# Attention scores made once, and their probabilities turned by DMA: one core, sixteen sequences

## The reference

```python
x = x + einsum(x, weight[subject]) + bias[subject]       # one of 8 matrices
x = x + diffusion(x)                                      # neighbours in both directions, and x * (1 - x)
# attention: 16 heads of 16 features, queries from a side input, 256 keys from x, and one key of the query's own
score_prev = einsum('bhqd,bhkd->bhqk', q, k_prev) / 4     # masked past seq_len1
score_self = (q * k_self).sum(-1) / 4
weights = softmax(concat[score_prev, score_self])
x = x + (weights[:-1] @ v_prev + weights[-1] * v_self) @ Wo + bo
# experts: relu(x @ wi) @ wo for two shared experts and one of 3 chosen, mixed by a gate of 3
x = x + eo * w[0] + s0 * w[1] + s1 * w[2]
```

## Time and profile before

| what | value |
|---|---|
| median of the runs | 1002.32 us |
| the profiled execution's own time | 998.3 us |
| its span, first to last instruction | 995.7 us |
| mean granted TensorE clock | 0.997 |
| PE busy | 972.3 us (98%), 9659 matmuls |
| DVE busy | 796.9 us (80%) |
| ACT busy | 686.8 us (69%) |
| POOL busy | 635.9 us (64%) |
| DMA | 82.71 MB, mean 83 GB/s; queue q1 28.2% of the 16 engines' time |

### The profile page before, as it was taken

The page is one execution under the profiler, slowest core; times in us unless marked ns, Lnnn a source line. Parts: engine busy times, 40 slices in busy tenths (PEclk is TensorE's granted clock), DMA queues, the critical chain, the costliest instruction groups (busy, mean ns, idle before and its releaser), DMA issues.

```text
span 995.7 us, 28043 instructions
## 1 busy us (share of the span) xinstructions
PE 972.3 (98%) x9659; PEld 932.9 (94%) x9659; DVE 796.9 (80%) x1566; ACT 686.8 (69%) x1442; POOL 635.9 (64%) x544
## 2 busy tenths in 40 slices
PE   7889999999999999999999999999999999999997
PEld 7779999999999999999999999999999999999997
DVE  6877887888888787878888788788888878787754
ACT  5776858677685876768577685867768587676742
POOL 5867747576685757658565774757668575765541
PEclk9999999999999999999999999999999999999999
DMA  7443232313214231231413123231321423122110
GB/s 211 140 118 96 65 108 63 95 54 106 85 43 127 64 95 53 81 110 43 114 53 114 58 63 108 63 95 54 106 85 43 126 64 95 53 84 76 45 54 11
DMA packets 92029, 82.71 MB, mean 83 GB/s; under 512 B 12100, under 2 KB 90980, under 8 KB 92004
## 3 DMA queue, kind: packets, MB, share of 16 engines
q1 hardware_dynamic: 91572, 81.99, 28.2%
q10 hardware_dynamic: 432, 0.39, 0.1%
HBM read 52.59 MB, written 4.20 MB: 57 GB/s over the span
## 4 chain that ended last, share of the span: by engine, by line
PE 75%; POOL 9%; issue 8%; DVE 3%; ACT 3%; SPq 1%; DMA 1%; POOLq 0%; ACTq 0%; DVEq 0%
PE out L721 8%; PE out L722 8%; PE hid L721 8%; PE out L723 8%; PE hid L722 7%; PE hid L723 7%; PE front L847 4%; PE front L833 4%; PE front L721 4%; PE front L723 3%; PE front L722 3%; POOL prob_lo L1607 3%; POOL exp_lo L1543 2%; PE pv L788 2%; PE pv L789 2%
## 5 line engine op out<-in xcount | busy, mean ns | idle before, releaser
L721 PE MATMUL hid<-x_hi,exp_hi 128*128 128x256 f32 x768 | 230.6, 300 | 0.2
L721 PE MATMUL out<-hid_hi,exp_hi 128*128 128x256 f32 x768 | 229.0, 298 | 0.0
L1607 POOL TENSOR_TENSOR prob_lo<-prob,prob_hi 128x512 f16<-128x512 f32 x141 | 182.6, 1296 | 61.5 <-ACT prob_hi L1121 61.4
L722 PE MATMUL out<-hid_lo,exp_hi 128*128 128x256 f32 x768 | 217.3, 283 | 0.0
L723 PE MATMUL out<-hid_hi,exp_lo 128*128 128x256 f32 x768 | 216.8, 282 | 0.0
L722 PE MATMUL hid<-x_lo,exp_hi 128*128 128x256 f32 x768 | 216.5, 282 | 0.0
L723 PE MATMUL hid<-x_hi,exp_lo 128*128 128x256 f32 x768 | 216.2, 282 | 0.0
L1294 DVE TENSOR_REDUCE s_max<-front 128x2 f32<-128x512 f32 x247 | 163.5, 688 | 60.8 <-PE front L833 58.8
L1543 POOL TENSOR_TENSOR exp_lo<-raw,exp_hi 128x512 fp32r<-128x512 f32 x128 | 168.8, 1334 | 60.1 <-ACT exp_hi L1138 60.0
L1160 ACT ACTIVATE hid_hi<-hid 128x512 fp32r<-128x512 f32 x192 | 115.7, 603 | 101.2 <-PE hid L723 100.0
L1117 ACT ACTIVATE prob<-front 128x512 f32<-128x512 f32 x246 | 148.6, 604 | 24.2 <-PE front L847 20.6
(11 more groups left out here) (269 smaller groups left out, 2334.4 us busy)
## 6 DMA issues: line engine op xcount, KB each, us to landing
raw<-in_wi SPq DMA_DIRECT2D x64, 256.0 KB, 3.8
raw<-in_wo SPq DMA_DIRECT2D x64, 256.0 KB, 2.7
q_rows<-w_raw SPq DMA_DIRECT2D x80, 128.0 KB, 2.4
k_rows<-x_raw SPq DMA_DIRECT2D x48, 128.0 KB, 2.4
k_rows<-x1T SPq DMA_DIRECT2D x45, 128.0 KB, 2.3
x_raw<-in_x SPq DMA_DIRECT2D x16, 256.0 KB, 3.1
w_raw<-in_w SPq DMA_DIRECT2D x16, 256.0 KB, 2.7
s_raw<-in_side SPq DMA_DIRECT2D x16, 256.0 KB, 3.4
```

The source lines that it names most:

```text
L721: nc.tensor.matmul(acc, w_hi, a_hi, start=first, stop=False)
L722: nc.tensor.matmul(acc, w_hi, a_lo, start=False, stop=False)
L1607: nc.gpsimd.tensor_tensor(prob_lo[:, h % NPROB, :], prob[:, h % NPROB, :], prob_hi[:, h % NPROB, :], ALU.subtract).then_inc(prob_split_poo ...
```

## The change

- Stage E on PE, the maxima's way through PE, ScalarE and DMA (m0, m1, top0, top1) and pvend are gone.
- DVE takes the negated maximum of each head (L1294 before); ScalarE takes the exponential from the bank of stage S, with the query on the partitions and the maximum as its bias, in two halves of 256 columns. Stage C is a copy of prob (SBUF) to fp16. The factor 1/4 moves into the queries.
- SP stage T: for each head one transposing DMA of the high part (128 x 512, fp16) as soon as C is done, and one of the low part once that is made. There are three buffers of parts, and three of turned parts, one of them ksT's. Between its waits SP raises semaphores.
- `attend` is a PE stage V of its own, which waits for both DMAs.
- The maximum doesn't include the own score: own0 and own1 make two weights from the difference (one for the own term, one for all the others), and half, norm and att multiply by the second.
- All lists are in new orders. The opening has 190 idle matmuls in place of 132.

```diff
 PE_BODY = """
-H0 H1 S0 S1 P0 S2 S3 H2 S4 S5 P1 S6 S7 H3 S8 P2 m0 H4 S9 S10 P3 S11 H5
-E0 S12 P4 E1 S13 H6 E2 S14 P5 E3 S15 H7 E4 E5 P6 E6 H8 m1 E7
-x1 P7 q E8 H9 E9 lap P8 E10 E11 H10 E12 kp E13 P9 E14 E15 H11 P10 pvend P11
-vs aT ks gate wo logits vp self
+H0 H1 S0 S1 P0 H2 S2 P1 S3 H3 S4 P2 H4 S5 S6 V0 P3 H5 S7 V1 V2 P4 x1 S8 V3 H6 P5 S9 V4 S10 H7 V5 V6 q S11 P6 S12 V7 H8 P7 S13 S14 V8 V9
+H9 H10 S15 V10 P8 lap V11 V12 P9 H11 kp P10 V13 V14 V15 P11 vs aT ks gate wo logits vp self
...
 SP_BODY = """
-wo0 wo1 m0 wo2 wo3 m1 wi_load E15 kp k3 load sum
+T0 T1 T2 T3 wo0 T4 T5 T6 wo1 T7 T8 T9 wo2 T10 T11 T12 wo3 T13 T14 T15 kp k3 load wi_load sum
...
-NPROB = 3
+NPROB = 2
+NPARTS = 3
+NTURNED = 3
...
+                elif name[0] == "T":
+                    h = int(name[1:])
+                    if h == NTURNED - 1:
+                        wait_filled(sp, i, "self")
+                        sp.sem_inc(self_seen, 1)
+                    wait(sp, pv_done, H, i, max(h - NTURNED + 1, 0))
+                    sp.sem_inc(values_seen, 1)
+                    wait(sp, hi_done, H, i, h + 1)
+                    sp.sem_inc(hi_seen, 1)
+                    sp.dma_start(turned[h % NTURNED][:, 0:2 * C], prob_parts[:, h % NPARTS, 0], transpose=True).then_inc(turned_in[h % NPARTS], 16)
+                    wait_prob_split(sp, i, h)
+                    sp.sem_inc(parts_seen, 1)
+                    sp.dma_start(turned[h % NTURNED][:, 2 * C:4 * C], prob_parts[:, h % NPARTS, 1], transpose=True).then_inc(turned_in[h % NPARTS], 16)
...
             def attend(i, h):
 
-                wait_prob_split(pe, i, h)
+                wait_turned(pe, i, h)
...
-                    for k in range(C):
-                        last = nc.tensor.matmul(psum[:, k * S:(k + 1) * S], k_rows[0:ROWS_EXP, h, k * P:(k + 1) * P],
-                                                q_rows[0:ROWS_EXP, h, :], start=True, stop=True)
...
                 elif name[0] == "E":
                     h = int(name[1:])
-                    wait_filled(act, i, name)
+                    wait(act, max_done, H, i, h + 1)
                     if h >= NPROB:
                         wait_prob_split(act, i, h - NPROB)
-                    psum = front_psum(name, i)
-                    last = nc.scalar.activation(prob[:, h % NPROB, :], psum[:, :], ACT.Exp, scale=SCALE)
-                    if h not in HI_DVE:
-                        if h >= NPROB:
-                            wait(act, pv_done, H, i, h - NPROB + 1)
-                        last = nc.scalar.activation(prob_hi[:, h % NPROB, :], psum[:, :], ACT.Exp, scale=SCALE)
-                    last.then_inc(freed["E"], 1)
+                    psum = chunked(front_psum(f"S{h}", i))
+                    for t in range(C):
+                        last = nc.scalar.activation(prob[:, h % NPROB, t * S:(t + 1) * S], psum[:, t, :], ACT.Exp, bias=neg_max[:, t, h:h + 1])
+                    last.then_inc(freed["S"], 1)
+                elif name[0] == "C":
+                    h = int(name[1:])
+                    wait_freed(act, i, f"S{h}")
+                    wait_turned(act, i, h - NPARTS)
+                    nc.scalar.activation(prob_parts[:, h % NPARTS, 0, :], prob[:, h % NPROB, :], ACT.Copy).then_inc(hi_done, 1)
...
+                    weighted = of_step(nc.vector.tensor_tensor(den[:, :, heads], sums[:, :, :, 3 * DH], c_prev[:, :, heads], ALU.mult))
...
+                        summed[t] = of_step(nc.vector.tensor_tensor(by_head(t), by_head(t), spread(c_prev, t), ALU.mult))
```

More of the change, by code:

```diff
@@ L62 @@
 """.split()
 ACT_BODY = """
-H0 wi0 H1 x3_keep wi1 H2 wi2 wi3 H3 m0 wo0 H4 P3 wo1 x_parts H5 E0 w_parts wo2 E1 H6 E2 wo3 E3 H7 E4 E5 E6 m1 H8 s_parts E7
-x1_parts react P7 q E8 H9 E9 x2_parts qa E10 E11 H10 E12 kp E13 E14 E15 H11 qb kq P11
-aT vs ks x3_parts logits vp x2b sum
+H0 x_parts w_parts H1 E0 E1 C0 C1 H2 wi0 E2 wi1 C2 wi2 H3 E3 E4 C3 s_parts H4 C4 E5 P3 C5 E6 H5 E7 C6 wi3 wo0 C7 E8 H6 C8 react E9 own0
+C9 E10 H7 wo1 q C10 x1_parts E11 x3_keep E12 C11 C12 H8 wo2 E13 P7 H9 qa C13 E14 C14 E15 C15 x2_parts wo3 H10 own1 qb H11 kp kq P11 aT
@@ L67 @@
+ks vs logits x3_parts vp sum x2b
 """.split()
 DVE_BODY = """
-H0 S0 S1 H1 S2 S3 S4 S5 H2 S6 S7 top0 S8 H3 S9 S10 H4 S11 gate0a S12 H5 S13 E1 S14 H6 S15 E3 top1 H7 gate0b x_parts E5 H8
-x1 E7 x1_parts react lap H9 half x2_parts E11 kp H10 E13 gate1 E14 H11
-att k3 gate2 aT relu wo logits x3_parts mix scale vp self
+H0 S0 S1 H1 S2 H2 E1 S3 S4 x_parts H3 E3 S5 H4 S6 S7 E5 gate0a H5 S8 own0 x1 E7 S9 S10 H6 E9 H7 S11 S12 x1_parts half E11 S13 H8 S14
+react S15 E13 H9 lap own1 x2_parts H10 gate0b H11 gate1 kp att gate2 aT k3 relu wo logits mix x3_parts scale self vp
@@ L72 @@
 """.split()
 POOL_BODY = """
-wi0 wi1 wi2 wi3 wo0 m0 x_parts wo1 E0 w_parts wo2 E2 wo3 E4 E6 s_parts x1 E8 m1 E9 E10 qa E12 norm E15 qb ks vp sum
+E0 x_parts wi0 E2 w_parts s_parts E4 wi1 wi2 E6 E8 wi3 wo0 wo1 E10 x1 E12 wo2 qa E14 E15 wo3 own norm qb ks sum vp
 """.split()
 SP_BODY = """
-wo0 wo1 m0 wo2 wo3 m1 wi_load E15 kp k3 load sum
+T0 T1 T2 T3 wo0 T4 T5 T6 wo1 T7 T8 T9 wo2 T10 T11 T12 wo3 T13 T14 T15 kp k3 load wi_load sum
 """.split()
-S_OF, E_OF = [f"S{h}" for h in range(H)], [f"E{h}" for h in range(H)]
+BY_HEAD = [f"{kind}{h}" for kind in "SECTV" for h in range(H)]
@@ L81 @@
 PRESENT = "x_parts w_parts s_parts x1 x1_parts react q qa qb lap x2_parts ks vs kp kq k3 vp x2b self".split()
-PREVIOUS = S_OF + E_OF + "m0 m1 top0 top1 half norm pvend att aT wo x3_parts wi_load".split()
+PREVIOUS = BY_HEAD + "own0 own1 own half norm att aT wo x3_parts wi_load".split()
 def lag(name):
     return -1 if name == "load" else 0 if name in PRESENT else 1 if name in PREVIOUS else 2
-FAMILIES = {"S": H, "E": H, "m": 2, "x1": 1, "q": 1, "lap": 1, "ks": 1, "vs": 1, "kp": 1, "vp": 1, "self": 1}
@@ L91 @@
-ACT_FREES = ("E", "m", "q", "ks", "vs")
+FAMILIES = {"S": H, "x1": 1, "q": 1, "lap": 1, "ks": 1, "vs": 1, "kp": 1, "vp": 1, "self": 1}
 def family(name):
@@ L128 @@
-shared2 E7 shared4 half kp.1 E11 E13 E14 E15 att k3.1 aT wo x3_parts vp.1 self.1
+memsets x_lo w_lo s_lo laps x_parts x1 beside x1_parts react bias_q lap setup x2_parts bias_k kp k3 vp S0 S1 S2 S3 shared2 E1 self S4
+S5 S6 S7 E3 S8 E5 x_parts.1 S9 own0 x1.1 E7 x1_parts.1 react.1 S10 S11 E9 half S12 S13 S14 E11 lap.1 x2_parts.1 S15 E13 own1 kp.1 E15
+shared4 att k3.1 aT wo x3_parts vp.1 self.1
 """))
 OPEN_POOL = list(opening("""
-memsets lin0 lin1 qa lin2 qb lin3 ks shared0 shared1 vp shared3a maxima shared3b w_parts.1 x_parts.1 s_parts.1 E0 E2 x1.1 E4 m1 E6 E8 E9 E10
@@ L136 @@
+k3.1 load.2 wi_load gates
 """))
@@ L161 @@
-H8.15 P7.15 H9.15 H10.15 H11.15 logits.15 first.15
+wi0 H0 wi1 E0 C0 E1 H1 C1 E2 C2 H2 E3 E4 wi2 C3 C4 H3 E5 H4 C5 x3_keep wi3 E6 C6 E7 P3 C7 own0 E8 wo0 H5 C8 E9 C9 E10 H6 C10 E11 wo1 H7
+E12 C11 C12 wo2 E13 H8 C13 P7 E14 C14 H9 E15 C15 wo3 own1 H10 H11 P11 aT x3_parts H0.15 wi0.15 H1.15 logits wi1.15 H2.15 sum wi2.15
+wi3.15 wo0.15 wo1.15 H3.15 H4.15 P3.15 H5.15 H6.15 wo2.15 H7.15 H8.15 P7.15 H9.15 H10.15 wo3.15 H11.15 logits.15 first.15
 """))
 CLOSE_DVE = list(closing("""
-H0 S0 S1 H1 S2 S3 S4 S5 H2 S6 S7 top0 S8 H3 S9 S10 H4 S11 S12 H5 gate0a S13 E1 S14 H6 S15 top1 E3 H7 gate0b E5 H8
@@ L165 @@
-E7 half H9 E11 E12 E13 H10 E14 E15 att H11 aT wo x3_parts gate1 gate2
-H0.15 relu H1.15 logits mix H2.15 scale H3.15 ones.15 H4.15 gate0a.15 H5.15 H6.15 H7.15 gate0b.15 H8.15 base.15 H9.15 gate1.15
-H10.15 first.15 H11.15 y_cols.15 second0.15 relu.15 second1.15 logits.15 mix.15 last.15
+S0 H0 S1 S2 H1 E1 S3 S4 H2 E3 S5 H3 S6 E5 S7 H4 own0 S8 E7 S9 H5 S10 E9 S11 S12 H6 half H7 S13 E11 E12 S14 E13 H8 S15 gate0a H9 own1
+E15 gate0b H10 gate1 H11 att aT gate2 wo x3_parts relu H0.15 logits mix H1.15 scale H2.15 H3.15 H4.15 H5.15 gate0a.15 gate0b.15 base.15
@@ L168 @@
+H6.15 H7.15 H8.15 H9.15 gate1.15 first.15 H10.15 H11.15 y_cols.15 ones.15 second0.15 second1.15 relu.15 logits.15 mix.15 last.15
 """))
 CLOSE_POOL = list(closing("""
-wi0 wi1 wi2 wi3 wo0 m0 wo1 E0 wo2 E2 wo3 E4 m1 E6 E8 E9 E10 norm
-wi0.15 wi1.15 sum wi2.15 wi3.15 wo0.15 wo1.15 wo2.15 wo3.15
+E0 E2 wi0 wi1 E4 E6 wi2 wi3 E8 E10 wo0 wo1 wo2 E14 wo3 own norm wi0.15 wi1.15 sum wi2.15 wi3.15 wo0.15 wo1.15 wo2.15 wo3.15
 """))
 CLOSE_SP = list(closing("""
-wo0 wo1 wo2 m0 wo3 m1 wi_load E15 wo0.15 wo1.15 sum wo2.15 wo3.15 sum.15
+T0 T1 T2 wo0 T3 T4 T5 wo1 T6 T7 wo2 T8 T9 T10 wo3 T11 T12 T13 T14 T15 wi_load wo0.15 wo1.15 sum wo2.15 wo3.15 sum.15
@@ L410, in build @@
         max_done = sem("max_done")
-        max_split = sem("max_split")
+        hi_done = sem("hi_done")
+        turned_in = [sem(f"turned{n}_in") for n in range(NPARTS)]
+        hi_seen = sem("hi_seen")
+        parts_seen = sem("parts_seen")
+        self_seen = sem("self_seen")
+        values_seen = sem("values_seen")
         d_self_done = sem("d_self_done")
@@ L786, in attend @@
                     for k in range(C):
[L787 to L790, removed]
```

(16 more changed lines are left out.)

202 lines of the change are left out of this document (88 added, 114 removed).

## The result

The changed kernel takes 1192.51 us (median of 2, 1190.08 to 1194.94) against 1002.32: 1.191 times as long, 95% interval 1.185 to 1.197. The profiled execution takes 1190.08 us with a span of 1188.2, which is 192.5 us more than before.

The account below looks back on a forecast made before the run. PE was taken to bound the loop: a turn falls from 59.12 to 56.2 us, 41 us less over 14 turns, closing 3 less, opening 4 more, so 40 us less: 962 us, range 947 to 1070.

Parts of the forecast that it names:

- What bounds the kernel now: In the middle of the loop PE is the bound, busy 58.76 of 59.00 us; a turn is 59.12 us.
- what PE loses and gains: Per loop turn PE loses 4.1 us of work and gains 0.7 at stage V: net 3.4 us less (3.2 to 3.7).
- I take 0.9 us, waits and raised semaphores included: SP's time for issuing one transposing DMA in stage T, with bounds 0.4 and 1.8 us.
- the SP rival: Each turn, V15 comes late by 32 times an issue's excess over 1.05 us on SP; slower, chance 0.21.
- What is allowed: 1.0 to 1.05 us each: From T0 to V15 SP has 36 us for 32 transposing and 4 wo DMAs, so issues of 0.9 us fit.
- SP becomes the bound: SP's in-order queue holds up the loop if an issue costs over 1.05 us; about 1080 at 1.3 us; chance 0.21.
- 4 wo 3.3: The four wo loads in a turn were taken to hold SP for 3.3 us, 0.8 each.
- Landing "2.4": A transposing DMA in stage T lands 2.4 us after its issue, like a plain one of the same 128 KB.
- A page's rule as a mechanism here: Transposing DMAs move their four 128 x 128 blocks one after another, holding SP and buffers: about 1870 us; chance 0.02.
- A wait at aT: Before transposing the result, PE waits for DVE's longer att: 0.5 us late each turn (0 to 0.7).
- Opening ... I take 4 (0 to 7): The opening gets 4 us longer (0 to 7), from 58 more idle matmuls less the removed stage E.

Follow-up runs that it names:

- the combined kernel: The changed kernel with one transposing DMA per head, the expert's number read once a turn, and SP's opening placings in the order of before: 969.78 us, 0.971.
- the best version: The changed kernel with one transposing DMA per head, one expert reading a turn, SP's old opening order, and wo ahead of vp.1 in PE's opening: 967.63 us, 0.969.

## Why the prediction was wrong

The forecast (962 us) and the range (up to 1070) missed 1192.5. By the steps of the prediction:

- **What bounds the kernel now; what PE loses and gains.** Right for the kernel before, and right in sign for PE's work. Where SP doesn't hold PE up, in the combined kernel, a turn is 55.5 us with 0.8 us of waiting before aT, so without that wait it fell by 59.1 - 54.7 = 4.4 us; I had a net of 3.4 (3.2 to 3.7). Even with no loss at the change from short to wide matmuls my terms give 4.1. What the rest is, no run shows.
- **"I take 0.9 us, waits and raised semaphores included".** This is the step that failed, and with it the sentence that 32 such DMAs fit beside PE's work. An issue alone is 1.19 us, and with its waits and raises 1.41 per DMA (1.38 and 1.44 in turn). The rows ended at 0.89 and I took their upper end for the operation that none of them showed. My own bound was 1.8, and the range, which ended at 1070, should have carried it: at 1.41 the SP rival's formula gives 56.2 + 32 x (1.41 - 1.05) = 67.7 us a turn, 70.3 with the 2.6 us of the wo loads (below), and 69.9 was measured.
- **"What is allowed: 1.0 to 1.05 us each".** Near the truth, by luck in its parts. V0 to V15 is 31.9 us in the combined kernel, not 34, and the items that I named add up to no more than that; but T0 starts 3.3 us behind S0 in the changed kernel, not 6. The rival *SP becomes the bound* names the place, the mechanism and the sign; it had 0.21.
- **"4 wo 3.3".** Also low: a wo load costs 1.46 us on SP, not 0.8. In the earlier trace rows x2 took 1.63, which is two issues of 0.4 with only one reading of the expert's number between them; the other reading lies ahead of the row. The four wo loads take 2.6 us a turn more than I had.
- **Landing "2.4".** Right: 2.5 (median).
- **A page's rule as a mechanism here.** Out. The Trainium skill's 1309 ns for a 128 x 128 block by DMA (VectorE: DVE Perf Modes, The three transpose paths) doesn't add up by block: eight blocks land after 3.1 us and hold SP for 1.24. The Trainium skill, Advanced Engine Details and Errata (X-Bar Transpose), says that transposing DMAs are as fast as regular ones. The traces agree roughly for the landing (2.5 us against 2.0 for a plain one of the same bytes) and not for the issue (1.19 against 0.49 us), which is what counted.
- **"A wait at aT", 0.5 us.** It is hidden in the changed kernel, where PE is late anyway, and 0.8 to 0.9 us a turn once SP is out of the way: my upper end was 0.7.
- **"Opening ... I take 4 (0 to 7)".** Wrong: 28 us in the changed kernel. With one DMA per head 23 are left. SP's order ahead of the first S was 3.5 of them (it brought S0 forward by 6, H0 by 3.5), and without the idle matmuls H0 comes 6 us earlier, though neither shows in the medians. In the best version 17 are left: 12 to 13 from the first S to aT, 4 to 5 from aT to H0. The granted clock of the opening (40 to 90 us) is 0.76 there, against 1.00 in the earlier trace rows; how much of the 17 us that is stays open.

## What to carry to other kernels

A DMA has a price at the engine that issues it, apart from its bytes and its landing; where many small ones stand in one queue, that price times their number is the first sum to make. If no row shows the operation, a nearby operation's row isn't a bound on it: carry the wide end into the range, or measure it first. And before reordering work to remove a wait, ask where the wait will go: in all three tries here one stood somewhere else afterwards. And when an issue's cost is fixed, join transfers, even if the joined one must wait for its last part: here 16 DMAs of 256 KB a turn make the kernel 211 us faster than 32 of 128 KB.

## What the runs showed of the hardware

- A transposing DMA from SBUF to SBUF holds SP for 1.19 us at 128 x 512 fp16 and for 1.24 us at 128 x 1024; a plain one of the first size for 0.49. They land after 2.5, 3.1 and 2.0 us.
- Reading the expert's number from SBUF into a register of SP costs 0.8 us of its time in the changed kernel (the load itself 0.26 to 0.50), a raise of a semaphore 0.07, of which its row shows 17 ns.
- An exponential of 128 x 256 from PSUM with a bias by partition takes 467 ns (median of 494), where the copies of that size in the earlier trace rows take 377 (mean). Two of them for one of 604 ns cost ScalarE more than was counted, at no loss here.
- The granted clock was 0.95 in a turn of the changed kernel, in which PE was busy for 60.0 of 69.4 us, and 1.00 with one DMA per head (55.1 of 56.3). In that turn it was 0.50 from 571.7 to 578.5 us, after 27 us in which PE was busy for 18.8; there PE waits for SP anyway. It costs time where it falls behind T15, as from 513.7 to 517.1: such turns take 69.9 us or more from T0 to T0, those without 68.9 to 69.3. So the waiting costs a second time, by 0.8 to 0.9 us in 10 of the 14 turns.
